# Talking-heads mix behind the softmax: tiles of 64 rows by 128 keys in place of quarters of 64 by 64

## Time and profile before

| | |
|---|---|
| median of 3 runs | 5096.99 us (5095.61 to 5101.71) |
| span of the profiled execution | 5096.0 us |
| PE busy | 4967.6 us, 97% |
| PE weight loads busy | 4084.3 us, 80% |
| DVE busy | 3402.4 us, 67% |
| ACT busy | 3103.6 us, 61% |
| POOL busy | 2880.2 us, 57% |
| instructions | 184542 |

### The profile page before, as it was taken

How to read it: one execution, slowest core, us unless ns; L and a number is a source line. 1 busy time by engine, 2 the same in 40 slices (tenths; PEclk the granted TensorE clock), 3 DMA queues, 4 the chain that set the end, 5 groups by cost and what they waited for, 6 DMA issues and landing times. The chain is left out here.

```text
span 5096.0 us, 184542 instructions
## 1 busy us (share of the span) xinstructions
PE 4967.6 (97%) x76184; PEld 4084.3 (80%) x76184; DVE 3402.4 (67%) x8316; ACT 3103.6 (61%) x8073; POOL 2880.2 (57%) x2509
## 2 busy tenths in 40 slices
PE   7999999999999999999999999999999999999998
PEld 5887878878888888887887878888888888878886
DVE  7667676666766667666676766767667676676764
ACT  4656665566655666556666556665566665666655
POOL 5546565565655656555565554655546565465654
PEclk9999999999999999999999999999999999999999
DMA  2311112121111211112111211212112112111111
GB/s 86 120 72 66 70 54 75 47 69 64 55 74 46 75 58 55 74 61 68 50 67 62 74 55 53 80 47 74 55 62 70 47 74 78 44 64 70 53 60 30
DMA packets 61263, 325.85 MB, mean 64 GB/s; under 512 B 6416, under 2 KB 23824, under 8 KB 43536
## 3 DMA queue, kind: packets, MB, share of 16 engines
q1 hardware_dynamic: 49632, 297.26, 15.5%
q0 software_dynamic: 10800, 16.78, 1.7%
HBM read 288.33 MB, written 34.08 MB: 63 GB/s over the span
## 5 line engine op out<-in xcount | busy, mean ns | idle before, releaser
L1603 POOL TENSOR_TENSOR q_lo<-q_mix,q_hi 128x512 fp32r<-128x512 f32 x512 | 661.6, 1292 | 886.5 <-ACT q_hi L1059 886.4
L1072 ACT ACTIVATE probs<-bank_S,neg_max 128x512 f32<-128x512 f32 x1024 | 699.3, 684 | 727.7 <-DVE neg_max L1333 630.1
L772 PE MATMUL bank_S<-k_hi,q_lo 128*128 128x512 f32 x2048 | 880.0, 430 | 22.8 <-ACT probs L1072 13.5
L1333 DVE TENSOR_REDUCE neg_max<-bank_S 128x1 f32<-128x512 f32 x1024 | 696.0, 686 | 277.1 <-PE bank_S L774 269.7
L773 PE MATMUL bank_S<-k_lo,q_hi 128*128 128x512 f32 x2048 | 806.7, 394 | 0.5 <-issue 0.5
L774 PE MATMUL bank_S<-k_hi,q_hi 128*128 128x512 f32 x2048 | 806.3, 394 | 0.0
L789 PEld LDWEIGHTS bank_M<-mixer_n,probs 64*64 64x64 f32 x32768 | 534.0, 135 | 151.5 <-issue 132.9
L1598 POOL TENSOR_TENSOR q_mix<-q_rope,w_pre 128x256 f32<-128x256 f32 x1024 | 625.4, 638 | 43.8 <-POOL q_lo L1603 0.4
L789 PE MATMUL bank_M<-mixer_n,probs 64*64 64x64 f32 x32768 | 600.1, 221 | 8.6 <-DVE o_locT_lo L1442 3.4
L1629 POOL TENSOR_TENSOR l_probs<-l_probs,l_inv 128x1024 f32<-128x1024 f32 (+1 forms) x256 | 430.6, 1689 | 265.7 <-DVE l_inv L1436 265.1
L1614 POOL TENSOR_TENSOR inv_norms<-norms_c,minus_half 128x16 f32<-128x16 f32 x128 | 417.1, 3259 | 239.3 <-DVE norms_c L1370 237.5
(11 more groups left out here) (160 smaller groups left out, 11381.3 us busy)
## 6 DMA issues: line engine op xcount, KB each, us to landing
w_qkv_hi<-split_qkv SPq DMA_DIRECT2D x30, 1536.0 KB, 9.7
w_qkv_lo<-split_qkv SPq DMA_DIRECT2D x30, 1536.0 KB, 6.4
w_hi<-split SPq DMA_DIRECT2D x30, 1408.0 KB, 6.2
w_lo<-split SPq DMA_DIRECT2D x30, 1408.0 KB, 6.1
w_hi<-split SPq DMA_DIRECT2D x30, 768.0 KB, 5.1
w_lo<-split SPq DMA_DIRECT2D x30, 768.0 KB, 7.2
w_o_hi<-split_o SPq DMA_DIRECT2D x30, 512.0 KB, 3.7
w_o_lo<-split_o SPq DMA_DIRECT2D x30, 512.0 KB, 4.7
```

Source lines behind the costliest of these rows:

```text
L772: mm(bank[k][:], q_lo[q], k_hi[:, s, :], start=(s == 0), stop=False)
L1072: fn(probs[:, n % PB, :], bank[k][:], ACT.Exp, bias=neg_max[:, n % 2:n % 2 + 1], accum_out=row_sum[:, n % 4:n % 4 + 1]).then_inc(emptied[k ...
L1333: v.tensor_reduce(neg_max[:, n % 2:n % 2 + 1], bank[k][:], AX.X, ALU.max, negate=True)\
L1603: g.tensor_tensor(q_lo[:, c % QB], q_mix[:], q_hi[:, c % QB].bitcast(F32), ALU.subtract)\
```

## The change

The loop over the two halves of the keys goes. One matmul has 64 rows by 128 keys as its stationary operand and writes all 128 partitions of the bank. The moving operand, the banks, the columns and the semaphores are as before.

```diff
                         for r in range(RH):
                             rows = slice(r * (P // RH), (r + 1) * (P // RH))
                             at = (t * TW + j) * GH * HI
-                            for half in range(2):
-                                keys = slice(half * (P // 2), (half + 1) * (P // 2))
-                                last = mm(bank[f"M{r}"][keys, at:at + GH * HI],
-                                          probs[rows, (2 * m + t) % PB, j * P + keys.start:j * P + keys.stop],
-                                          mixer_n[rows, m % 2, t, :], start=True, stop=True)
+                            last = mm(bank[f"M{r}"][:, at:at + GH * HI], probs[rows, (2 * m + t) % PB, j * P:(j + 1) * P],
+                                      mixer_n[rows, m % 2, t, :], start=True, stop=True)
                             if t and j == TW - 1:
                                 last.then_inc(filled[f"M{r}"], 1)
```

## The result

The changed kernel takes 5500.79 us (median of 4 runs, 5497.11 to 5503.24) where the kernel before took 5098.12 us (5095.61 to 5101.71). The ratio is 1.0787, 95% interval 1.0771 to 1.0803: slower by 403 us. 5525 us was forecast, with 5450 to 5590 as the range.

A forecast was written before the change was run, and what follows sets the result against it. PE was taken to set the pace. 5096.0 + 436.6 (longer rounds in `mix`) + 22 (borders) - 30 (waits given back) = 5524.6 us, forecast as 5525 us, with 5450 to 5590 as the range.

The forecast's parts named there:

- PE's pace sets the time: Whole kernel: PE, busy in 97% of the span, sets the pace; what the change adds to PE's time, the span gains.
- The round: In `mix`: 16 rounds, each going from 58.3 to 111.6 ns as the 128-column load sets it; 436.6 us more.
- rival A: In `mix`: the two row tiles don't run side by side; 32 passes of 111.6 ns, about 6450 us; chance 0.05.
- rival B: In `mix`: 128-column loads are quick, 141 ns as in the transposes; 5100 to 5119 us; chance 0.05.
- The borders with `local_scores`: Between `mix` and `local_scores`: tile shapes now differ, 0.14 us lost at each of 157 borders, 22 us more.
- Given back: PE's own waits: some close as other engines get more time per `mix`; 30 us less, bounds 0 and 90.
- The bound of 90 us: PE's idle 128.4 us: some 25 are the start and 10 the tail, so 90 could close at most.
- rival C: In `mix`: PE's sequencer sets the pace at 7.3 ns an instruction; fewer instructions give about 4880 us; chance 0.04.
- rival D: In `mix`: load and stream of a tile come one after the other, rounds of 165 ns, 5962 us; chance 0.01.

The follow-up runs named there:

- doubled stream: Each matmul but a mix's last streams its 64 columns twice: in the kernel before 5422.48 us (1.065), in the changed kernel 5501.49 us (1.0806).
- quarters with their halves of the keys apart: Kernel before with the loop over the key halves outermost, its 64 by 64 matmuls kept: 5434.55 us, 1.0673.
- doubled quarters: Kernel before, its 64 by 64 tiles each moving their 64 columns twice, except the last of a mix: 5422.48 us, 1.065.
- eighths: Kernel before with eight tiles of 64 rows by 32 keys in place of its 64 by 64 ones: 5553.96 us, 1.0908.
- Quarters: The tiles of 64 by 64 in the kernel before, four side by side: 5098.12 us.
- halves that move their columns twice: Changed kernel with the moving operand doubled, 128 columns streamed to loads of 128: 5501.49 us, 1.0806.
- row tiles apart: Changed kernel with the loop over the row halves outermost, all matmuls of r = 0 and then all of r = 1: 6515.48 us, 1.2791.

## Why the prediction was right

Point by point, by its own steps:

- **PE's pace sets the time.** Right: 512 x 0.84 us and 157 x 0.14 us are 452 us more on PE, and 403 us came out.
- **The round.** Forecast 111.6 ns, and 111 ns seen, 16 rounds. The row that gave it was that of L953, a load of 128 columns with almost no stream. The doubled stream shows that the reason was right too: free beside a load of 128 columns, 333 us beside one of 64. The quarters with their halves of the keys apart show that it isn't the number of tiles. Per `mix` 0.853 us was forecast and 0.84 came; 7 us in all.
- **Two row tiles side by side** (rival A): they are, and only because they alternate in the program. Apart, they cost 28.4 rounds.
- **Quick wide loads** (rival B): no, 188 ns.
- **The borders with `local_scores`.** 0.14 us at each, as forecast: 2.74 us together where 1.93 and 0.81 are the parts. The traces show that it goes with the shape: the loads of `local_scores` start 0.16 us sooner behind `mix` than those of other steps where both have tiles of 64 by 64 (0.93 against 1.09 us before, 1.64 against 1.80 with the doubled quarters), and no sooner with tiles of 64 by 128 or 64 by 32. What PE does at such a change of shape, no run shows.
- **Given back.** This is the term of the sum that was mis-sized: 30 us forecast, 452 - 403 = 49 us measured. Of these, PE's idle time shows 35.3: 13.0 at `scores` for the exponential, 11.2 at `values` for nothing named (20.7 to 9.5, while its wait for ACT's copy rose by 8.9 to 12.9 us), and many small ones. Some 14 us more are not in PE's idle time, as the modelled ends of matmuls can cover a wait: the `mix` steps of before took some 28 us more in all than their common lengths, those of after some 10. I had kept back two thirds of what idle time I held to be open, because of waits that follow on PE's own last step. Two waits for engines that are behind closed nearly wholly, the exponential's and the 7.8 us at `local_scores` for DVE; the one for ACT's copy did not. I had not thought of the supply of instructions. It probably eased as the program got shorter (184542 to 151774 instructions): of the 19 stops at `values` over 0.5 us in the trace before, behind its first 400 us, 16 ended 1.2 to 1.6 us after an instruction packet had landed, and 6 of 21 after the change. The bound of 90 us was read wrongly from the earlier trace rows: the first window is idle for 36.2 us and the last for 24.6, which leaves 67.6 and not 90 for those between, and of these 31.1 closed (36.5 left after the change). The 19 us too few given back and the 7 us too many for the round are, to 2 us, the 24 us by which the forecast was high.
- **The sequencer** (rival C): wrong for this change, but the eighths show that its limit lies close. Quarters with a pair in 58.3/4 = 14.6 ns have room; at 7 ns a pair there is none.
- **Load and stream in turn** (rival D): no. The rule of the Trainium skill (TensorE: Matmul & The Clock Gate, Part 3: Packing small matmuls), that a load overlaps with matmuls in flight only where the row group differs, doesn't hold for this kernel's loads: the halves that move their columns twice have 111 ns a round with 107 ns of columns to load and as many to stream in the same row group. The same section of the Trainium skill, ahead of that rule, also lets a load into the background weight buffer go ahead of matmuls in flight. That allows the overlap that the trace shows; that it is this buffer, no run shows.

## What to carry to other kernels

Where PE sets the pace and a matmul moves few columns, count the columns of a weight load, not the matmuls: here a round (one pass on each of the tiles that run side by side) cost the longer of load and stream, and narrower tiles side by side divided the load. That paid only while tiles alternated closely in the program, and only until the pairs came faster than PE's program is handed out, which in this kernel was about 9.5 ns a pair in the mean. For the price of a shape that a trace doesn't have, look for a line, however rare, in which one of the two (load or stream) is alone.

## What the runs showed of the hardware

- PE overlaps a tile's passes with another tile's only if these come soon in the program. With tiles of 64 by 128 and long runs of one tile, 3.5 to 3.6 passes are saved at each change of tile (28.4 rounds with one change, 21.4 with three), with 64 by 64 three. With seven changes, runs of four passes, that is nearly enough for full overlap: 16.4 rounds where 16 are the least.
- The instructions of PE come in packets of 256 (65536 more made 256 packets more, of 16384 bytes each), and a stretch of short matmuls can outrun them: stops of up to 4.9 us for nothing that the profile names, 97 at `mix` in the eighths, and 89 of the 90 stops over 0.6 us inside a `mix` end 1.2 to 1.6 us after such a packet has landed.
- A PE that shows 99% busy can still lose its clock: with the row tiles apart, one tile of 64 rows at work for most of 3.3 us, the granted clock was 0.94 over the run, though PE's records left no gap there.
- Loads slow down with the clock too: a `mix` made of them took 6.23 us at the low level and 3.32 at the high one, and the record of a matmul with 512 columns went from 0.39 to 0.63 us. The changed kernel shows it too: its one `mix` at the low level, in batch 0, took 3.60 us where the others took 1.93.
